# A transformer block with attention and routed experts on one core: coefficients spread through memory, two head groups in one PSUM bank, merged masks, fewer waits, and a written order per engine

## The reference

```python
h = layernorm(x) * (1 + ca) + sa
q, k, v = h @ Wq + bq, h @ Wk + bk, h @ Wv + bv      # 16 heads of 8
att = softmax(causal(q @ k.T / sqrt(8)))
y = (att @ v) @ Wo + bo
x = x + ga * (layernorm(y) * gamma + beta)
h = layernorm(x) * (1 + cb) + sb
probs = softmax(h @ router)                          # 8 experts
coef = probs where among the top 2, else 0
routed = sum_e coef[:, e] * ((silu(h @ gate_e) * (h @ up_e)) @ down_e)
shared = (silu(h @ sg) * (h @ su)) @ sd
x = x + gb * (routed + shared)
```

## Time and profile before

| | us |
|---|---|
| median of 3 runs | 552.45 (551.6 to 552.94) |
| the profiled execution, its own time | 553.16 |
| its span, from first to last instruction | 551.4 |

### The profile page before, as it was taken

The page is one execution under the profiler, slowest core; times in us unless marked ns, Lnnn a source line. Parts: engine busy times, 40 slices in busy tenths (PEclk is TensorE's granted clock), DMA queues, the critical chain, the costliest instruction groups (busy, mean ns, idle before and its releaser), DMA issues.

```text
span 551.4 us, 10280 instructions
## 1 busy us (share of the span) xinstructions
PE 502.8 (91%) x3626; PEld 273.1 (50%) x3626; DVE 359.7 (65%) x806; ACT 292.2 (53%) x615; POOL 254.1 (46%) x366
## 2 busy tenths in 40 slices
PE   4478989999999999999999999999999998999867
PEld 2133444554655464555645464456455464546435
DVE  4464685688567757786668757784868755873055
ACT  2213554756467446756466646655575645655311
POOL 6034335724664266724663367525672433334500
PEclk9755996999999999999999999999999999999769
DMA  4682231411333114410341123410441131001000
GB/s 114 198 202 71 66 102 28 117 48 40 102 88 80 45 31 114 121 47 2 102 120 46 44 77 76 115 45 21 95 119 50 30 83 45 2 2 41 0 0 21
DMA packets 35795, 37.93 MB, mean 69 GB/s; under 512 B 8832, under 2 KB 30880, under 8 KB 35616
## 3 DMA queue, kind: packets, MB, share of 16 engines
q1 hardware_dynamic: 31508, 33.46, 23.8%
q10 hardware_dynamic: 4236, 3.81, 2.3%
HBM read 26.36 MB, written 10.50 MB: 67 GB/s over the span
## 4 chain that ended last, share of the span: by engine, by line
PE 68%; DVE 16%; ACT 7%; DMA 5%; issue 2%; SPq 1%; POOL 0%; DVEq 0%; POOLq 0%; ACTq 0%
PE s_bank L1233 11%; PE pv_bank L1265 10%; PE s_bank L1251 9%; PE gate_bank L1337 7%; PE up_bank L1348 7%; PE gate_bank L1380 6%; DVE row_max L1046 6%; PE s_bank L1235 4%; PE misc L1184 4%; ACT probs L860 3%; PE misc L1215 2%; DVE stats_x L994 2%; DMA k_stack<-k_scr 2%; PE up_bank L1289 2%; DMA q_stack<-max_rows 2%
## 5 line engine op out<-in xcount | busy, mean ns | idle before, releaser
L1046 DVE TENSOR_REDUCE row_max<-s_bank 128x1 f32<-128x512 f32 (+3 forms) x352 | 212.4, 635 | 57.0 <-PE s_bank L1235 54.7
L860 ACT ACTIVATE probs<-s_bank 128x512 f32<-128x512 f32 x320 | 181.5, 597 | 71.8 <-PE s_bank L1251 67.6
L1233 PE MATMUL s_bank<-k_stack,q_stack 72*128 72x256 bf16 (+3 forms) x512 | 136.4, 315 | 16.7 <-DMA q_stack<-q_scr 7.8
L1251 PE MATMUL s_bank<-q_stack,k_stack 75*128 75x128 bf16 (+3 forms) x512 | 118.0, 307 | 10.1 <-ACT probs L860 6.3
L728 POOL TENSOR_SCALAR_AFFINE_SELECT probs<-probs 128x512 f32<-128x512 f32 (+1 forms) x96 | 75.4, 791 | 97.8 <-ACT probs L860 97.1
L1235 PE MATMUL s_bank<-causal,ident_bf 128*128 128x128 bf16 x512 | 101.0, 227 | 0.0
L1265 PE MATMUL pv_bank<-probs,v_aug 128*32 128x512 f32 (+3 forms) x1024 | 90.6, 449 | 0.4 <-POOL probs L728 0.3
L1233 PEld LDWEIGHTS s_bank<-k_stack,q_stack 72*128 72x128 bf16 x512 | 51.7, 101 | 71.6 <-DVE row_max L1046 44.4
L1251 PEld LDWEIGHTS s_bank<-q_stack,k_stack 75*128 75x128 bf16 x512 | 42.3, 100 | 58.9 <-ACT probs L860 24.5
L1235 PEld LDWEIGHTS s_bank<-causal,ident_bf 128*128 128x128 bf16 x512 | 52.0, 102 | 16.6 <-issue 7.8
L713 POOL TENSOR_TENSOR hidden<-hidden,coef_sb 128x512 f32<-128x512 f32 x28 | 35.6, 1272 | 22.2 <-ACT coef_sb L914 22.2
(11 more groups left out here) (179 smaller groups left out, 574.7 us busy)
## 6 DMA issues: line engine op xcount, KB each, us to landing
k_stack<-k_scr SPq DMA_DIRECT2D x96, 96.0 KB
q_stack<-q_scr SPq DMA_DIRECT2D x93, 96.0 KB
k_scr<-k_parts SPq DMA_DIRECT2D x32, 96.0 KB, 1.9
q_scr<-q_parts SPq DMA_DIRECT2D x31, 96.0 KB, 1.9
k_scr<-k_parts SPq DMA_DIRECT2D x32, 64.0 KB, 1.8
x_res<-in_L_attn_x SPq DMA_DIRECT2D x8, 256.0 KB, 4.0
x_in<-in_L_attn_x ACTq DMA_DIRECT2D x7, 256.0 KB, 3.0
out_x<-out_sb SPq DMA_DIRECT2D x7, 256.0 KB, 2.6
```

Of the source, the lines that this page charges most:

```text
L860: nc.scalar.activation(dst, src, ACT.Exp, scale=SCALE).then_inc(exp_done, 1)
L1046: nc.vector.reduce_max(row_max[s % 2][:, 0, h:h + nh, qt], s1_bank[u % 2][:, 0:nh * w].rearrange("p (h k) -> p h k", h=nh), AX_X).then_inc ...
L1233: nc.tensor.matmul(dst[:, w * i:w * (i + 1)], q_stack[0:KROWS, h, P * qt:P * (qt + 1)], k_stack[0:KROWS, h, 0:w], start=True, stop=False)
L1251: final = nc.tensor.matmul(dst[:, at:at + w], k_stack[0:MROWS, hh, P * j:P * (j + 1)], q_stack[0:MROWS, hh, P * j:T], start=True, stop=True)
```

## The change

- **Coefficients.** For all batches but the last, the `c` products, their copies, and the three-part split are gone. `ct` turns the float coefficients into 8 rows in `misc`, ScalarE copies them to `coef_rows`, SyncE writes them to memory with every row stored eight times (`cw`, 64 rows of 2 KB), waits, and issues four reads (`cl`) which spread the 16 rows of two experts over 128 partitions of `coef_all`, 256 KB each. The multiply on GpSimd stays. The tail does as before.
- **Two groups in one bank.** An odd group reads its values through a window that starts 8 columns earlier, so that its 8 results and its sum of ones land beside those of the even group in the same 32 partitions, and it adds to the bank. Eviction, `o` and the wait for `u_ready` come once for two groups; the normalisation is one reciprocal and two products.
- **Masks.** The diagonal blocks of all heads of a unit take one product, with the mask repeated.
- **Down.** The product of zeros is gone; the first product of the bank starts the sum.
- **Waits.** `need_all` is gone with its waits on constants, and several others on things long done, or done earlier on the same path.
- **Order.** A list of tasks for each of the five engines in each of the four plans, in place of time line and shifts.

```diff
 ORDER = {
...
     "middle": {
...
+        "pe": ("pv.0.1 s2.0.0 s2.0.1 pv.0.2 s1.0.0 s1.0.1 s2.0.2 pv.0.3 s1.0.2 s2.0.3 s1.0.3 s2.0.4 s1.0.4 s2.0.5"
+              " s1.0.5 s2.0.6 s1.0.6 s2.0.7 s1.0.7 s2.0.8 s1.0.8 s2.0.9 s1.0.9 xt s1.0.10 pv.0.0 s1.1.0 q s1.1.1"
+              " s1.1.2 pv.1.1 s1.1.3 pv.1.2 max.0 pv.1.3 s1.1.4 k s1.1.5 s1.1.6 s2.1.0 s1.1.7 s2.1.1 s1.1.8 s2.1.2"
+              " o.1 s1.1.9 s2.1.3 s1.1.10 s2.1.4 ot s2.1.5 s1.2.0 s2.1.6 y s1.2.1 max.1 s1.2.2 s2.1.7 s1.2.3 s2.1.8"
+              " pv.1.0 s1.2.4 s1.2.5 s2.1.9 v s1.2.6 pv.2.1 s1.2.7 s1.2.8 pv.2.2 s2.2.0 s2.2.1 s1.2.9 pv.2.3 s2.2.2"
+              " s2.2.3 s1.2.10 s2.2.4 s1.3.0 s2.2.5 s1.3.1 s2.2.6 s1.3.2 s2.2.7 max.2 s1.3.3 s2.2.8 pv.2.0 s2.2.9"
+              " s1.3.4 x2t s1.3.5 pv.3.1 s1.3.6 s1.3.7 lg pv.3.2 g0 pv.3.3 s1.3.8 s2.3.0 s1.3.9 s2.3.1 u0 o.3 s2.3.2"
+              " g1 s2.3.3 s2.3.4 u1 ct g2 u2 s1.3.10 s2.3.5 s2.3.6 g3 s2.3.7 u3 s2.3.8 max.3 s2.3.9 g4 u4 pv.3.0"
+              " down0 down1 down2 down3 down4"),
...
+        "pool": ("wdb xs xn s2.0.3 s2.0.7 ot s2.0.9 msplit.0 q k s2.1.3 msplit.1 ystat s2.1.7 s2.1.9 x2stat msplit.2"
+              " s2.2.3 s2.2.7 s2.2.9 msplit.3 s2.3.3 s2.3.7 c0 c1 c2 c3 s2.3.9"),
+        "sp": ("load.0 xres load.1 max.0 stack max.1 load.2 max.2 load.3 cw cl max.3 fin"),
     },
...
+                if name == "cw":
+
+                    sp.wait_ge(misc_read, misc_at(it, (s_of(it, "ct"), "ct", 0)) + 1)
+                    for landed in coef_landed:
+                        need(sp, landed, it * 16 - 16)
+                    sp.dma_start(coef_scr, coef_rows[:, :].unsqueeze(1).to_broadcast([E, COPIES, T])).then_inc(coef_written, 16)
+                if name == "cl":
+                    sp.wait_ge(coef_written, it * 16)
+                    need(sp, weighted, it * FB - FB)
+                    for a in range(FB):
+                        rows = coef_scr[2 * a:2 * a + 2].rearrange("e r t -> (e r) t").unsqueeze(1).to_broadcast(
+                            [2 * COPIES, DE // COPIES, T])
+                        sp.dma_start(coef_all[:, a, :], rows).then_inc(coef_landed[a], 16)
...
                 if name == "c" and not last(it):
 
-                    pool.wait_ge(misc_read, misc_at(it, (s, "c", a)) + 1)
+                    pool.wait_ge(coef_landed[a], it * 16)
                     pool.wait_ge(up_read, it * MB + (a + 1 - MB))
-                    nc.gpsimd.tensor_tensor(hidden[:, a, :], hidden[:, a, :], coef_sb[:, :], ALU.mult).then_inc(weighted, 1)
+                    nc.gpsimd.tensor_tensor(hidden[:, a, :], hidden[:, a, :], coef_all[:, a, :], ALU.mult).then_inc(weighted, 1)
...
                 if name == "s2" and a in SELECT_AFTER:
 
                     pr = probs[(s - 1) % G % 2]
-                    need_all(pool, (const_done, 1), (exp_done, it * (G * U2) + U2 * (s - 1) + a + 1))
+                    pool.wait_ge(exp_done, it * (G * U2) + U2 * (s - 1) + a + 1)
...
+                if name == "ct" and not last(it):
+                    act.wait_ge(misc_written, misc_at(it, (s, "ct", 0)) + 1)
+                    need(act, coef_written, it * 16 - 16)
+                    nc.scalar.activation(coef_rows[:, :], misc[0:E, :], ACT.Copy).then_inc(misc_read, 1)
...
                         nc.tensor.matmul(dst[:, w * i:w * (i + 1)], q_stack[0:KROWS, h, P * qt:P * (qt + 1)],
-                                         k_stack[0:KROWS, h, 0:w], start=True, stop=False)
-                        final = nc.tensor.matmul(dst[:, w * (i + 1) - P:w * (i + 1)], ident_bf[:, :], causal[:, :],
-                                                start=False, stop=True)
-                    final.then_inc(s1_written, 1)
+                                         k_stack[0:KROWS, h, 0:w], start=(i == 0), stop=False)
+                    diagonal = dst[:, 0:nh * w].rearrange("p (h k) -> p h k", h=nh)[:, :, w - P:w]
+                    nc.tensor.matmul(diagonal, ident_bf[:, :], causal[:, :].unsqueeze(1).to_broadcast([P, nh, P]),
+                                     start=False, stop=True).then_inc(s1_written, 1)
...
                     if a == 0:
-                        need(pe, u_ready, it * G + (s - 1))
-                        wait_v(pe, it - (s == 0), misc_read, v_read)
+                        if g % PAIR == 0:
+                            need(pe, u_ready, it * PAIRS + n // PAIR)
+                        if n == 0:
+                            wait_v(pe, it, misc_read, v_read)
+                    odd = g % PAIR
+                    values = v_aug[(it - (n < 0)) % 2][:, j, :, :].rearrange("p h v -> p (h v)")
                     for h in range(GH):
-                        final = nc.tensor.matmul(pv_bank[VC * h:VC * (h + 1), P * j:T], v_aug[(it - (n < 0)) % 2][:, j, GH * g + h, :],
+                        at = VC * (GH * g + h) - DH * odd
+                        final = nc.tensor.matmul(pv_bank[VC * h:VC * (h + 1), P * j:T], values[:, at:at + VC],
                                                 probs[g % 2][:, h, P_AT[j]:P_AT[j] + T - P * j],
-                                                start=(a == 0), stop=(a == len(PV_ORDER) - 1))
-                    if a == len(PV_ORDER) - 1:
+                                                start=(a == 0 and not odd), stop=(a == len(PV_ORDER) - 1 and odd == 1))
+                    if a == len(PV_ORDER) - 1 and odd:
                         final.then_inc(pv_done, 1)
...
-                if name == "c" and not last(it):
-                    take_misc(it, (s, "c", a))
-                    nc.tensor.matmul(misc[:, :], pick[:, a, :, :].rearrange("p a b -> p (a b)"), coef_T[:, :],
-                                     start=True, stop=True).then_inc(misc_written, 1)
                 if name == "down":
...
-                        for bank, w in ((s2_bank[0], T // 2), (s1_bank[0], T // 2)) if last(it) else ((gate_bank, T),):
-                            nc.tensor.matmul(bank[:, 0:w], zero_row[:, 0:P], zero_row[:, 0:w], start=True, stop=False)
```

250 lines of the change are left out of this document (86 added, 164 removed), and 123 rows, old and new, of the table ORDER.

## The result

The changed kernel takes 549.22 us (median of 20 runs, 542.28 to 554.99) where the kernel before takes 552.7 (20 runs, 548.83 to 559.63): a ratio of 0.9903, 95% interval 0.9873 to 0.9932. The medians are over all runs, while every ratio in this document, and so the gain of 5.4 us by this one, is of fast runs alone, and the profiled execution (551.37 us, a span of 549.5) is one of the changed kernel's slow ones. The forecast was 21 us.

What follows compares the result with a forecast made beforehand. TensorE, busy 91% of the span, was taken to bound the middle. Six steady batches at -2.7 us, last attention batch -2.6, first -1.0, tail -1.2 gave -21.0, so 531.5 us; own range 527 to 537, full range 522 to 545.

Steps and rivals of the forecast that it cites:

- What bounds the kernel: Steady batches: TensorE busy 58.85 of 60.52 us, about 2.6 us of stalls; the ends are chains with waits.
- zero product: Product of zeros opening the `down` sum on TensorE: removal saves 0.31 us a batch, at least 0.2.
- masks: Merged mask products on TensorE: 20 fewer instructions a batch, same columns, saving 0.1 us a batch.
- removed waits: Waits on constants and long finished loads: bounds 0 and 0.3 us a batch, taken as 0.
- Sum for TensorE and its stalls: Steady batch: TensorE's own work -0.9 us, stalls -1.8, together -2.7, to a period of 57.8 us.
- the +1.0 for the list: TensorE's new middle order: 16 lone `pv` runs instead of 12 runs, 0.24 us each, adding 1.0 us a batch.
- New path of the coefficients: Transfers from `ct` to the multiplies before `down`: last multiply ends at 11.1 us, wanted about 12.5; nothing added.
- Rival 3: Coefficient loads land in 9.8 us, 5.4 us late, net +2.7 in seven batches: 569 us; chance 0.05.
- Ends: Last attention batch -2.6 us (0.7 of it stalls), first batch -1.0, tail -1.2, start unchanged.
- rival 1: TensorE: only the work goes, the stalls stay; -8.8 us, 543.6 us; chance 0.22.
- rival 2: The order packs better, stalls nearly vanish: -3.5 us a batch, -26.7 in all, 525.7 us; chance 0.16.
- rival 4: Mask products cost by record length: 35 us more gain, 496 us; chance 0.01.

Runs made afterwards that it cites:

- all three lists: The task orders of the kernel before, the changed kernel, and the changed kernel with `pv` steps joined to 11 runs a batch, the last measured at 549.63 us.
- the constant: Changed kernel, GpSimd multiplying by a constant tile instead of `coef_all`, waiting for no landing, transfers still issued: period 57.53 us, median 533.87 us, ratio 0.968.
- the kernel with cut loads: Changed kernel with each coefficient row stored once and each 256 KB load cut in two, one per expert: 532.43 us, ratio 0.962.

## Why the prediction was wrong, step by step

- *What bounds the kernel*: right. The prices from start times that were tried hold: zero product (0.31 read, 0.33 measured), masks (0.1 and 0.08), a `pv` run (0.15 behind it in all three lists). So does nothing for the removed waits.
- *Sum for TensorE and its stalls*: right in total, 57.8 forecast and 57.53 with the constant, but partly by luck, since two errors cancel. Counted from start to start, with each idle row and its tail of 0.16 as a stall, the stalls went from 2.2 us to 1.1 (0.40 and 0.35 are left), so 1.2 less and not 1.8. TensorE's own work went from 58.3 to 56.5, so 1.8 less and not 0.9. The removed pieces account for it as priced (the four `pick` products 0.86, the `u_sb` transposes of two `o` steps 0.91, zero product 0.31). What fails is the +1.0 for the list: all that isn't one of the priced pieces came to +0.1. `pv` takes 0.3 us more and the products ahead of its runs 0.09 each, as read, but the products of gate, up, q, k and y take 0.8 us less. In the old order several stood beside runs of `pv`, as at 250.9, where the first gate product took 0.53 us to the next start instead of 0.43. So moving a run moves a cost as well; no run tests this by itself. (The prediction counts seven lone runs in the old order; the trace has nine, which gives its sum of 12.)
- *New path of the coefficients, "Nothing added"*: this step failed. The write was priced at 1.9 us from a write of like size, and took 4.34; the loads at 3.0 for the first with the others following, and they took 3.5 with a gap of 0.9. Together the last coefficient came 3.9 us later than forecast, against a slack of 1.4, so 2.5 us were added to every batch where the step had nothing. The fault was to carry a duration over by bytes when the shape was another: `k_parts` leaves from 32 partitions, `coef_rows` from 8, and from 32 the same bytes took 1.95.
- *Rival 3* had the right mechanism at the wrong place and size: it made the loads slow, where the write was, and its 5.4 us of lateness were 2.5. Since that is below the 2.7 from which the rival decides, the kernel stayed faster. Its sign to look for, GpSimd idle for a DMA and TensorE idle over 0.5 before `down`, came as written: 0.35 and 1.00 for GpSimd. With a slack of 0.3 to 1.4 us under a write and four loads never seen in the trace, 1 in 20 was too little, and the range ought to have taken in the write at bounds of its own, as it did only for the loads.
- *Ends*: the last attention batch gains 1.4 us with the constant (58.63 to 57.23), not 2.6, and loses 0.9 in the changed kernel, since its coefficients are late too. The step took 0.7 us of its stalls as gone; in the kernel with cut loads they stand there yet, these among them:

```profile
450.50 0.66 PE L1087 MATMUL misc<-ident,o_tok 128*128 128x128 f32 x4 [0.58 <-DVE o_tok L961]
454.72 0.88 PE L1154 MATMUL s_bank<-q_stack,k_stack 75*128 75x128 bf16 x4 [0.51 <-ACT probs L772]
...
460.17 0.39 PE L1136 MATMUL s_bank<-k_stack,q_stack 72*128 72x512 bf16 x1 [0.60 <-DVE row_max L949]
```

  The first batch and the tail (+2.2 and -2.4 us against a forecast of -1.0 and -1.2) can't be judged, for the clock differs (see below), and 1.9 of the +2.2 are late coefficients within that first `down`.
- *The other rivals*: the stalls did not stay (rival 1), nor did they nearly vanish (rival 2, 57.0), and masks don't go by records (rival 4).

## What to carry to other kernels

Price a transfer by one of its own shape, above all by how many partitions or rows stand in front on each side, and look at the DMA share while it runs: a share that sits just under 2/16 or 8/16 is a transfer that uses so many engines. Cutting the loads from memory by that sign gave more here (57.8 us a batch) than starting the chain earlier (58.4). Then divide the GB/s by the engines at work: where each of them is slow too, as in the reads from one, two or eight partitions of SBUF, more engines need not help, and the source is the thing to spread. Where a change puts a chain of transfers under a slack of one or two us, set the chance by that slack, since everything else in the sum can be right and the gain still go. And removing mode switches was worth nothing here, since the moved pieces were what TensorE did while another engine caught up. Last, check a sum term by term after the fact: this one was right to 0.3 us with two terms off by 0.6 to 0.9.
